# Second attention layer of a graph network: the two sums of the own rows move from GpSimd to VectorE

## The chip, the cores and the metric

One core of a Trainium2 chip runs the whole program in one launch. The metric is device time in microseconds (us). Five engines work side by side, each on its own in-order queue, and meet only at semaphores: TensorE (PE in the profile; PEld is its weight load), VectorE (DVE), ScalarE (ACT), GpSimd (POOL) and SyncE (SP, whose queue only issues transfers).

## The reference, cut to what matters

Four graph layers follow one another over 50,000 nodes of 128 features and 25,000 edges, sorted by destination. After each layer comes `x = layernorm(x + layer(x))`. The change lies in the third layer of the reference, the program's second attention layer (in the kernel `kind == 2`):

```python
q = x @ Wq + bq; k = x @ Wk + bk; v = x @ Wv + bv            # 8 heads of 16
score = einsum(q[dst], k[src]) / sqrt(16) + edge_attr @ We + be
exp_s = exp(score - segment_max(score, dst)[dst])
attn = exp_s / (segment_sum(exp_s, dst)[dst] + 1e-8)
out = segment_sum(attn * v[src], dst) @ Wo + bo
h = out + x                                                  # "own rows" are these x, one for each edge slot
layer = layernorm(h) * gamma + beta
x = layernorm(x + layer)
```

So the own row of a destination is needed twice: as `x + bo`, to which `out` is added before the first normalisation, and as `x + beta`, to which the scaled first normalisation is added before the second.

## The kernel before, in words

Nodes without edges are worked out in an early stage. The later stages work on edges in 49 chunks of 512 edge slots (`G_CH`; a chunk is a tile of 128 partitions x 512 columns, four blocks of 128 rows). Chunk L uses buffers `B[L % 5]` (`RING` is 5). The stage of `kind == 2` runs from about 2790 to 3675 us of the span, then comes a meeting of all engines and the stage of `kind == 3`, the last one.

Within a stage the order of each engine's queue is not written out by hand. Each step has a place in `plan`, and one iteration is `lag` places long (138 for this stage). `Line.run` (from L865 on) sorts the steps that an engine has by `place + lag * L` and issues them in that order. So an engine's round, in order of the place modulo 138, is in this stage:

- VectorE: `d.scale` (5), `maximum` (11), `h_res` (41), `d.stats` (50), `x3_pre` (64), `e.stats` (80), `sums` (94), `e.scale` (114), `qk` (120), `divide` (132)
- TensorE: `turn_o` (9), `turn_q` (22), `rows_o` (28), `turn_x` (38), `products` (84), `values` (101), `turn_sums` (117), `scores` (129)
- ScalarE: the copies out of PSUM, the exponentials and the applications of the normalisations
- GpSimd: `residual` (30) and `gather` (-420, over three rounds ahead)

Steps of different chunks share a round: `h_res` of chunk L runs about two rounds after `qk` of chunk L.

Steps that matter here, with the lines of the profile:

- `gather` (L900) issues eight indirect DMAs for a chunk: four of source rows (`gs`) and four of own rows (`own`). It first waits until chunk L-5 has gone through `xsT_ps`, `xdT_ps`, `xo` and `x2b`, since its buffers are written again.
- `residual` (GpSimd, L1773 and L1774) waits for the chunk's edge attributes (`ea_in`) and its gathered rows, then makes `xo = own + bo` and `w = own + beta2`. Each is a 128x512 float32 addition.
- `sums` (VectorE, L953, L957, L960) makes the messages and runs two scans, `den` and `num`.
- `turn_sums` (TensorE, L368, L1883, L965) turns `num` and `den` into rows as soon as `num` is there. `divide` (VectorE, L2023, L973, L975, L978) waits for it. L2023, the first instruction of that step, copies a few columns of chunk L-3 (`q_all`).
- `scores` (TensorE, L1856, L1858), `maximum` (VectorE, L931, L933, L935, L936, L938), `turn_o`, `turn_q` and `rows_o` (TensorE, L368, L374) follow. `h_res` (VectorE, L2039) adds `xo` to the product with `Wo` in PSUM, so it waits for `rows_o` and for `xo`. `x3_pre` (L2047, L2050) adds `w`.
- In the stage of `kind == 3` VectorE makes its own residual (L2059) as one 128x512 addition of the same form, beside gathers of GpSimd.

At the start of the stage the places put `gather` of chunks 0 to 3 ahead of `residual` of chunk 0 in GpSimd's queue.

Of the kernel before, what the change touches and what calls it, by code (L numbers as in the profile page):

```python
# [19 lines left out]
ALU = mybir.AluOpType  # L20
# [8 lines left out]
RING = 5  # L29
# [18 lines left out]
def build(nc, x, src, dst, ea32, ea64, ew, w, out):  # L48
# [65 lines left out]
    bo, gamma2, beta2 = (sb(n, [P, D]) for n in ("bo", "gamma2", "beta2"))  # L114
# [16 lines left out]
    def rows4(t):  # L131

        return t.rearrange("p (j f) -> p j f", j=SUB)

    def each_row(row):
        return row[:, None, :].to_broadcast([P, SUB, D])
# [854 lines left out]
    with ExitStack() as tmp:  # L991
# [9 lines left out]
        own = tile("own")  # L1001
# [672 lines left out]
    for kind in (2, 3):  # L1674
# [2 lines left out]
        table, ea = tables[kind + 1], (ea32 if kind == 2 else ea64)  # L1677
        if kind == 2:
            lag, plan = HOP4_LAG, {
                "load": (1, "ea_in pen_in"), "residual": (30, "xo x2b"),  # L1680
                "turn_x": (38, "xsT_ps xdT_ps eaT_ps"), "copy_xT": (66, "xsT xdT eaT"), "products": (84, "k_ps q_ps"),
                "values": (101, "v_ps"), "copy_z": (112, "kb"), "qk": (120, "qk"), "scores": (129, "z_ps"),
                "maximum": (149, "M_first M dz Dm0 Dm"), "gather": (-420, ""), "exps": (181, "p F"),
                "sums": (232, "msg den num"), "turn_sums": (255, "num_rows"), "divide": (270, "dn rd divided"),
                "turn_o": (285, "oT_ps"), "copy_oT": (296, "oT"), "rows_o": (304, "wo_ps"), "h_res": (317, "h_res"),
                **ln_plan("d", 326, 394, 419, 439), "x3_pre": (478, "dg x3_pre"), **ln_plan("e", 494, 510, 528, 547),
                "store": (565, "stored"), "turn_q": (574, "x3T_ps"), "copy_q": (592, "x3T")}
        else:
            lag, plan = HOP5_LAG, {
                "load": (1, "ea_in pen_in ew_in q_in own_in"),  # L1690
                "turn_x": (72, "xsT_ps eaT_ps"), "copy_xT": (100, "xsT eaT"), "residual": (105, "xo"), "products": (136, "z_ps"),
                "gather": (-420, ""), "values": (163, "v_ps"), "copy_z": (174, "kb"), "qk": (218, "zl"),
                "maximum": (227, "M_first M dz Dm0 Dm"), "exps": (261, "p F"), "sums": (286, "msg den num"),
                "turn_sums": (342, "num_rows"), "divide": (403, "dn rd divided"), "x4_pre": (416, "x4_pre"),
                **ln_plan("f", 474, 490, 516, 522), "scatter": (540, "")}
        new_phase()
        with ExitStack() as tmp:
            hop = Line(tmp, f"t{kind}", plan, lag, "xsT pen kb qk p F den num msg xo " + ("xdT w" if kind == 2 else "own u x4"),
                      {"gs": (table, NT + GT, slot_idx), **({"own": (table, NT + GT, own_idx)} if kind == 2 else {})})
            B = hop.B  # L1700
# [19 lines left out]
            with nc.Block() as block:  # L1720
# [41 lines left out]
                @block.gpsimd  # L1762
                def _(pool):
                    step = hop.steps()

                    if kind == 2:
                        @step("residual")
                        def _(L):

                            b = B[L % RING]  # L1770
                            step.due_dma(pool, "ea_in", L)
                            hop.due_gathered(pool, L)
                            nc.gpsimd.tensor_tensor(rows4(b["xo"][:]), rows4(b["own"][:]), each_row(bo), ALU.add).then_inc(S("xo"), 1)  # L1773
                            nc.gpsimd.tensor_tensor(rows4(b["w"][:]), rows4(b["own"][:]), each_row(beta2), ALU.add).then_inc(S("x2b"), 1)  # L1774

                    @step("gather")
                    def _(L):
                        for name in ["xsT_ps"] + ["xdT_ps", "xo", "x2b"] * (kind == 2):
                            step.due(pool, name, L, RING)
                        hop.gather(pool, L)  # L1780

                    if kind == 3:
                        @step("scatter")
                        def _(L):

                            step.due(pool, "f_out", L)
                            for t in range(SUB):
                                k = L * SUB + t
                                pool.indirect_dma_start(out=out, out_offset=bass.IndirectOffsetOnAxis(ap=end_idx[:, k:k + 1], axis=0),  # L1789
                                                        in_=B[L % RING]["x4"][:, t * D:(t + 1) * D], in_offset=None,  # L1790
                                                        bounds_check=NODES - 1, oob_is_err=False).then_inc(pool_dma[f"scattered{L % RING}"], 16)

                    step.run()
                    hop.end_gathers(pool)
                    if kind == 3:
                        for L in range(G_CH - RING, G_CH):
                            pool.wait_ge(pool_dma[f"scattered{L % RING}"], 16 * SUB * (L // RING + 1))
# [166 lines left out]
                def _(v):  # L1964
                    V = nc.vector
                    step = hop.steps()
# [64 lines left out]
                        divide(v, step, b, L, K[4], K[5], heads, 1e-8 if kind == 2 else 1e-16, b["o"])  # L2031

                    if kind == 2:
                        @step("h_res")
                        def _(L):
                            b = B[L % RING]
                            step.due(v, "wo_ps", L)
                            step.due(v, "xo", L)
                            V.tensor_tensor(b["u"][:], K[7], b["xo"][:], ALU.add).then_inc(S("h_res"), 1)  # L2039

                        ln_vector(v, step, B, "d", "u", "h_res")

                        @step("x3_pre")
                        def _(L):
                            b = B[L % RING]
                            step.due(v, "d_out", L)
                            V.tensor_tensor(rows4(b["v"][:]), rows4(b["v"][:]), each_row(gamma2), ALU.mult).then_inc(S("dg"), 1)  # L2047
                            step.due(v, "dg", L)
                            step.due(v, "x2b", L)
                            V.tensor_tensor(b["u"][:], b["v"][:], b["w"][:], ALU.add).then_inc(S("x3_pre"), 1)  # L2050

                        ln_vector(v, step, B, "e", "u", "x3_pre")
                    else:
                        @step("residual")
                        def _(L):

                            b = B[L % RING]
                            step.due_dma(v, "own_in", L)
                            V.tensor_tensor(rows4(b["xo"][:]), rows4(b["own"][:]), each_row(bias3), ALU.add).then_inc(S("xo"), 1)  # L2059

                        @step("x4_pre")
                        def _(L):
                            b = B[L % RING]
                            step.due(v, "divided", L)
                            step.due(v, "xo", L)
                            V.tensor_tensor(b["u"][:], b["o"][:], b["xo"][:], ALU.add).then_inc(S("x4_pre"), 1)

                        ln_vector(v, step, B, "f", "u", "x4_pre")
# [43 lines left out]
```

## Time and profile before

| | us |
|---|---|
| median of 3 runs | 4333.93 |
| lowest, highest | 4331.24, 4335.06 |
| the profiled execution | 4329.79 |
| its span, first to last instruction | 4328.1 |
| busy in the span: PE, DVE, ACT, POOL | 2921.5, 3475.1, 2494.4, 2522.2 |

The profiled execution is 4.14 us under the median, and 1.69 us of it lie outside the span. A busy share over the whole span mixes stages with different limits, so this table cannot say what the stage of the change waits for. For that one reads the stretch from 2790 to 3675 us alone, first by window, then by wait, then instruction by instruction. The granted clock of TensorE is a share of its full 2.4 GHz: a stretch at 0.5 runs at 1.2 GHz.

### The profile page before, as it was taken

How to read it: one execution, taken by the hardware profiler on the slowest of the kernel's cores; microseconds unless marked ns; L12 is line 12 of the kernel's file. 1: busy time of each engine (PE TensorE's matmuls, PEld its weight loads, DVE VectorE, ACT ScalarE, POOL GpSimd, SP SyncE). 2: the span in 40 equal slices, each digit the busy share in tenths (PEclk: the TensorE clock that was granted, in tenths of full speed). 3: DMA queues.
4: the chain of work that ended last, by engine and by line, in shares of the span. 5: the costliest groups of instructions: out<-in, count | busy, mean ns of one | idle time of the engine just before them, and what ended most of it. 6: DMA issues, size and time to landing. Idle time of an engine off the chain costs nothing. (4 is left out here: it accounts for less than half of the span.)

```text
span 4328.1 us, 48774 instructions
## 1 busy us (share of the span) xinstructions
PE 2921.5 (68%) x12128; PEld 1943.4 (45%) x12128; DVE 3475.1 (80%) x8069; ACT 2494.4 (58%) x5486; POOL 2522.2 (58%) x2300
## 2 busy tenths in 40 slices
PE   5777767777673178874545545478888887677775
PEld 3544444454442034444545534345555554344443
DVE  5999999999998678875656679768777776788886
ACT  3777777777776256762323334446656565455554
POOL 6655555545450166626767767588666650766664
PEclk9998898888986578777767755577777776656555
DMA  4876666555553388854444456422222220333331
GB/s 114 178 186 186 185 190 187 186 190 187 187 181 132 103 246 255 252 165 124 152 128 151 152 164 198 154 62 72 66 68 64 67 62 28 106 88 87 92 95 49
DMA packets 383765, 599.12 MB, mean 138 GB/s; under 512 B 124231, under 2 KB 205296, under 8 KB 383486
## 3 DMA queue, kind: packets, MB, share of 16 engines
q1 hardware_dynamic: 313726, 482.99, 36.5%
q0 software_dynamic: 69760, 113.02, 10.5%
q8 instruction: 101, 1.65, 0.2%
q14 instruction: 178, 1.46, 0.1%
HBM read 312.45 MB, written 287.17 MB: 139 GB/s over the span
## 5 line engine op out<-in xcount | busy, mean ns | idle before, releaser
L1555 POOL DMA_INDIRECT gs_g<-table_xw,slot_idx x588 | 593.9, 1010 | 296.9 <-issue 263.7
L900 POOL DMA_INDIRECT gs_t<-table_x,slot_idx x392 | 421.5, 1075 | 300.8 <-issue 198.5
L495 POOL DMA_INDIRECT gs<-x,src_idx x200 | 224.2, 1121 | 441.1 <-DMA xd_rows<-gd 368.8
L368 PE MATMUL ps<-ident,gs_g 128*128 128x128 f32 x588 | 137.1, 377 | 363.2 <-DMA gs_g<-table_xw,slot_idx 363.2
L1593 ACT ACTIVATE hT_g<-u_g 128x512 f32<-128x512 f32 x147 | 92.5, 629 | 497.7 <-DVE u_g L1642 497.7
L1272 POOL DMA_INDIRECT slot_idx<-node_map,src_idx x200 | 242.8, 1214 | 190.9 <-DMA slot_idx<-node_map,src_idx 94.6
L1635 DVE TENSOR_TENSOR_SCAN agg_g<-same_seg,agg_g,ps 128x512 f32<-128x512 uint8 x147 | 188.0, 1279 | 173.9 <-PE ps L368 173.6
L483 POOL DMA_INDIRECT node_map<-slot_no,end_idx x200 | 278.8, 1394 | 60.9 <-issue 60.3
L1789 POOL DMA_INDIRECT out<-x_t,end_idx x196 | 205.6, 1049 | 169.6 <-ACT x_t L339 116.9
L368 PEld LDWEIGHTS ps<-ident,gs_g 128*128 128x128 f32 x588 | 90.0, 190 | 402.6 <-issue 352.0
L495 POOL DMA_INDIRECT gd<-x,dst_idx x200 | 215.4, 1077 | 60.9 <-issue 60.0
L1848 PE MATMUL ps<-xsT_t,Wv 128*128 128x512 f32 x196 | 152.3, 870 | 133.0 <-DVE msg_t L953 132.8
L900 POOL DMA_INDIRECT own_t<-table_x,own_idx x196 | 200.3, 1022 | 59.7 <-issue 59.7
L1630 DVE SCALAR_TENSOR_TENSOR own_g<-bs_row,root,own_g 128x128 f32<-128x128 f32 x588 | 167.2, 346 | 48.7 <-DMA own_g<-table_xw 48.2
L628 ACT ACTIVATE h1T<-ps,h_bias 128x512 f32<-128x512 f32 x49 | 33.7, 687 | 268.7 <-DVE nm L775 267.9
L1940 ACT COPY xsT_t<-ps 128x512 f32<-128x512 f32 x49 | 28.7, 585 | 250.3 <-PE ps L368 250.3
L596 ACT ACTIVATE x_b<-v_b,nm,rs 128x128 f32<-128x128 f32 x392 | 156.6, 497 | 19.4 <-DVE nm L775 19.4
L596 ACT ACTIVATE x_b<-s_b,nm,rs 128x128 f32<-128x128 f32 x392 | 156.8, 497 | 17.1 <-DVE nm L775 17.1
L596 ACT ACTIVATE hf_b<-hf_b,nm,rs 128x128 f32<-128x128 f32 x392 | 157.5, 514 | 2.4 <-DVE nm L775 2.4
L596 ACT ACTIVATE x_b<-t_b,nm,rs 128x128 f32<-128x128 f32 x392 | 157.4, 510 | 0.0
L374 PE MATMUL ps<-WS,hT_g 128*128 128x128 f32 x784 | 152.9, 362 | 5.5 <-ACT xw_g L1601 5.5
L1913 ACT COPY xsT_t<-ps 128x512 f32<-128x512 f32 x98 | 56.4, 576 | 171.8 <-PE ps L368 171.8
(362 smaller groups left out, 10071.3 us busy)
## 6 DMA issues: line engine op xcount, KB each, us to landing
table_xw<-xw_b SPq DMA_DIRECT2D x147, 512.0 KB, 5.4
table_x<-x_b SPq DMA_DIRECT2D x98, 512.0 KB, 2.7
own_g<-table_xw SPq DMA_DIRECT2D x147, 256.0 KB, 3.7
x_in<-x SPq DMA_DIRECT2D x49, 512.0 KB
out<-hf_b SPq DMA_DIRECT2D x49, 512.0 KB, 2.9
table_xw<-xw_g SPq DMA_DIRECT2D x98, 256.0 KB
pen_t<-pen_row SPq DMA_DIRECT2D x98, 256.0 KB, 4.1
xd_rows<-gd SPq DMA_DIRECT2D x50, 256.0 KB, 5.6
```

The source lines that it names most:

```text
L368: last = nc.tensor.transpose(to[0:width, j * P:(j + 1) * P], t[:, j * width:(j + 1) * width], ident[:])
L374: last = nc.tensor.matmul(to[:, j * D:(j + 1) * D], tT[:, j * P:(j + 1) * P], W[:], start=True, stop=bias_row is None)
L483: pool.indirect_dma_start(out=node_map, out_offset=bass.IndirectOffsetOnAxis(ap=end_idx[:, t:t + 1], axis=0), in_=slot_no[:, t:t + 1], in_ ...
L495: pool.indirect_dma_start(out=to[k % 3][:, j * D:(j + 1) * D], out_offset=None, in_=x, in_offset=bass.IndirectOffsetOnAxis(ap=of[:, n:n + ...
L596: last = nc.scalar.activation(to[:, k * D:(k + 1) * D], of(k), ACT.Identity, scale=r[:, n, k:k + 1], bias=b[:, n, k:k + 1])
L900: pool.indirect_dma_start(out=self.B[L % RING][g][:, t * D:(t + 1) * D], out_offset=None, in_=table, in_offset=bass.IndirectOffsetOnAxis(a ...
L1272: pool.indirect_dma_start(out=slot_idx[:, t:t + 1], out_offset=None, in_=node_map, in_offset=bass.IndirectOffsetOnAxis(ap=src_idx[:, t:t + ...
L1555: pool.indirect_dma_start(out=gs[c % 6][:, j * D:(j + 1) * D], out_offset=None, in_=tables[layer], in_offset=bass.IndirectOffsetOnAxis(ap= ...
L1630: V.scalar_tensor_tensor(out=blk, in0=bs_row[layer][:], scalar=root4[:, k:k + 1], in1=blk, op0=ALU.mult, op1=ALU.add).then_inc(S("own_bias ...
L1635: V.tensor_tensor_scan(agg[t % 3][:], same_seg[:, t * CH:(t + 1) * CH], T_X[t % 2], agg[(t - 1) % 3][:, CH - 1:CH], ALU.mult, ALU.add).the ...
L1789: pool.indirect_dma_start(out=out, out_offset=bass.IndirectOffsetOnAxis(ap=end_idx[:, k:k + 1], axis=0), in_=B[L % RING]["x4"][:, t * D:(t ...
L1848: nc.tensor.matmul(K[3], (Wv if kind == 2 else Wv3)[:], B[L % RING]["xsT"][:], start=True, stop=True).then_inc(S("v_ps"), 1)
```

## The change

The step `residual` of the stage `kind == 2` goes from GpSimd's list to VectorE's list, and from place 30 to place 130. That is behind `qk` (120) and ahead of `divide` (132) in the round. It no longer waits for `ea_in`. Both semaphores are now raised by VectorE, and `gather` waits for the same ones as before.

```diff
-                "load": (1, "ea_in pen_in"), "residual": (30, "xo x2b"),
+                "load": (1, "ea_in pen_in"), "residual": (130, "xo x2b"),
...
                 def _(pool):
                     step = hop.steps()
 
-                    if kind == 2:
-                        @step("residual")
-                        def _(L):
-
-                            b = B[L % RING]
-                            step.due_dma(pool, "ea_in", L)
-                            hop.due_gathered(pool, L)
-                            nc.gpsimd.tensor_tensor(rows4(b["xo"][:]), rows4(b["own"][:]), each_row(bo), ALU.add).then_inc(S("xo"), 1)
-                            nc.gpsimd.tensor_tensor(rows4(b["w"][:]), rows4(b["own"][:]), each_row(beta2), ALU.add).then_inc(S("x2b"), 1)
-
...
                     if kind == 2:
+                        @step("residual")
+                        def _(L):
+                            b = B[L % RING]
+                            hop.due_gathered(v, L)
+                            V.tensor_tensor(rows4(b["xo"][:]), rows4(b["own"][:]), each_row(bo), ALU.add).then_inc(S("xo"), 1)
+                            V.tensor_tensor(rows4(b["w"][:]), rows4(b["own"][:]), each_row(beta2), ALU.add).then_inc(S("x2b"), 1)
+
                         @step("h_res")
```

## Rows read from the trace of the kernel before

**Rows 1.** Windows (busy by engine, PE clock, DMA share, GB/s), middle of the stage
```profile
3220.00:3320.00 100.00, 84.81 (x336) 55.48 (x336) 74.20 (x140) 60.84 (x117) 63.00 (x58) 0.73 0.25 66
```

**Rows 2.** Waits from 2850 to 3600 us: us in total, times, longest
```profile
DVE q_all L2023 <- PE ps L965: 76.5, 43, 3.4
POOL xo_t L1773 <- DMA ea<-ea: 66.0, 32, 14.6
```

**Rows 3.** Groups of VectorE, 2850 to 3600 us: busy us, mean ns, idle before
```profile
L957 DVE TENSOR_TENSOR_SCAN den_t<-F_t,den_t,p_t 128x512 f32<-128x512 f32 x44 | 59.4, 1351 | 0.0
...
L936 DVE TENSOR_TENSOR F_t<-pen_t,M_t 128x512 f32<-128x512 f32 x44 | 47.9, 1088 | 0.0
L938 DVE TENSOR_TENSOR F_t<-F_t,M_t 128x512 f32<-128x512 f32 x44 | 39.2, 891 | 1.5
```

**Rows 4.** Tile xo of both stages: ns min/median/max, first and last start
```profile
L1773 POOL TENSOR_TENSOR xo_t<-own_t,bo x49: 1256/1280/1795, 2833.6 to 3599.7; 128x512 f32<-128x512 f32 x49
...
L2059 DVE TENSOR_TENSOR xo_t<-own_t,bias x49: 681/684/693, 3700.6 to 4285.9; 128x512 f32<-128x512 f32 x49
```

**Rows 5.** Timeline of VectorE, one round: start us, us, engine, instruction, [idle before]
```profile
3269.69 1.26 DVE L960 TENSOR_TENSOR_SCAN num_t<-F_t,num_t,msg_t 128x512 f32<-128x512 f32 x1
...
3271.13 0.75 DVE L2006 SCALAR_TENSOR_TENSOR qk_t<-ps,bq,kb_t 128x512 f32<-128x512 f32 x1
3273.38 0.17 DVE L2023 COPY q_all<-ps 128x16 f32<-128x16 f32 x1 [1.50 <-PE ps L965]
```

**Rows 6.** Timeline of VectorE, the last stage's residual and what follows it
```profile
3961.49 0.68 DVE L2059 TENSOR_TENSOR xo_t<-own_t,bias 128x512 f32<-128x512 f32 x1
3962.09 0.17 DVE L329 RECIPROCAL rs_t<-sd_t 128x4 f32<-128x4 f32 x1
```

**Rows 7.** Timelines of VectorE and GpSimd, last full rounds of the stage
```profile
3595.85 0.18 DVE L973 TENSOR_SCALAR dn_t<-ps 128x32 f32<-128x32 f32 x1
...
3600.89 1.28 POOL L1774 TENSOR_TENSOR w_t<-own_t,beta 128x512 f32<-128x512 f32 x1
...
3612.90 0.18 DVE L973 TENSOR_SCALAR dn_t<-ps 128x32 f32<-128x32 f32 x1
...
3620.80 0.69 DVE L2039 TENSOR_TENSOR F_t<-ps,xo_t 128x512 f32<-128x512 f32 x1 [0.85 <-PE ps L374]
...
3629.95 0.18 DVE L973 TENSOR_SCALAR dn_t<-ps 128x32 f32<-128x32 f32 x1
```

**Rows 8.** Timelines of three engines at the start of the stage
```profile
2825.83 1.16 PE L374 MATMUL ps<-Wo,xsT_t 128*128 128x128 f32 x8 [0.68 <-ACT xsT_t L1940]
...
2827.58 0.69 DVE L938 TENSOR_TENSOR F_t<-F_t,M_t 128x512 f32<-128x512 f32 x1
...
2832.61 1.00 POOL L900 DMA_INDIRECT own_t<-table_x,own_idx  x1 [0.30 <-issue]
2833.64 1.27 POOL L1773 TENSOR_TENSOR xo_t<-own_t,bo 128x512 f32<-128x512 f32 x1
...
2835.01 0.69 DVE L2039 TENSOR_TENSOR F_t<-ps,xo_t 128x512 f32<-128x512 f32 x1 [6.74 <-POOL xo_t L1773]
```

**Rows 9.** Line L900, every gather: time from issue to landing
```profile
DMA to landing us min/median/max: 2.4/2.6/6.2
```

**Rows 10.** Timelines of GpSimd and VectorE, a long scan in the fourth round
```profile
2887.89 1.28 POOL L1773 TENSOR_TENSOR xo_t<-own_t,bo 128x512 f32<-128x512 f32 x1
...
2889.11 2.39 DVE L957 TENSOR_TENSOR_SCAN den_t<-F_t,den_t,p_t 128x512 f32<-128x512 f32 x1
```

**Rows 11.** Timeline of VectorE, the first step of divide of chunk 1
```profile
2842.23 0.19 DVE L973 TENSOR_SCALAR dn_t<-ps 128x32 f32<-128x32 f32 x1 [2.07 <-PE ps L965]
```

**Rows 12.** Timeline of VectorE, one short round and a long operation in it
```profile
3273.47 0.18 DVE L973 TENSOR_SCALAR dn_t<-ps 128x32 f32<-128x32 f32 x1
...
3278.43 1.67 DVE L938 TENSOR_TENSOR F_t<-F_t,M_t 128x512 f32<-128x512 f32 x1
...
3289.20 0.18 DVE L973 TENSOR_SCALAR dn_t<-ps 128x32 f32<-128x32 f32 x1
```

## The prediction

> **What bounds the kernel now.** Of the span of 4328.1 us only the stage of the second attention layer, from 2790 to 3675 us, is touched, so I read that stretch alone. The windows come first: in the middle of the stage TensorE is busy 85 us of 100 at a granted clock of 0.73 of 2.4 GHz, VectorE 74, GpSimd 63 [rows 1]. No engine is full, so the rounds are set by a loop through several engines. The waits show where that loop holds VectorE. VectorE waits 76.5 us for TensorE before it copies the columns of `q_all` (43 times, 1.78 each) [rows 2]. GpSimd waits 66 us for the edge attributes: it is early, and no bottleneck in the steady part [rows 2].
>
> The timeline shows the first of these waits. `num` starts at 3269.69 and takes 1.26; TensorE can only then begin `turn_sums`. VectorE has `e.scale` and `qk` meanwhile, ends `qk` at 3271.88 and stands idle for 1.50 until 3273.38 [rows 5]. From the twelfth round on no round has less than this 1.50, and most have just that. That gap is the place to which the change moves the two additions.
>
> The round takes 17.05 us at the end of the stage, twice in a row (3595.85, 3612.90, 3629.95), and over the 46 rounds from 2842.23 to 3629.95 it is 787.72 / 46 = 17.12 on average [rows 7, 11]. Single rounds go from 15.7 (3273.47 to 3289.20) [rows 12] to about 18: TensorE alternates between its two clock levels, 1.2 and 2.4 GHz, within each round.
>
> **The change part by part.**
>
> *Added on VectorE, steady part.* Two 128x512 additions for each of 49 chunks. The nearest row is the same instruction form in the last stage: 681 to 693 ns, median 684, beside gathers [rows 4]. There the next instruction starts 0.60 after it [rows 6]. So two cost about 0.60 + 0.68 = 1.28 us per round: 49 x 1.28 = 63 us of VectorE work. It lies after `qk`. The first starts at about 3271.80, the second ends at about 3273.08, and the copy wanted by 3273.38 is not late: 0.3 us are left. On the path: 0. This cover is TensorE's `turn_sums`. If it were gone, up to 63 us would appear. The lower bound of the cost is 0 (additions cannot shorten the wait); the upper one comes from L936 and L938, which take up to about 1.0 longer when GpSimd adds at the same time [rows 12]: 2 x 1.0 less the 0.3 left is 1.7 a round, 78 us. I take 0, because the nearest row, L2059, never exceeds 693 ns and GpSimd no longer adds; the end of 78 needs an addition on GpSimd that the change removes, so only a small part of it enters the range.
>
> *Removed from GpSimd, steady part.* 98 additions of 1.28 us [rows 4], some 125 us of an engine that is early. On the path: 0 by itself. But they lengthen VectorE's work. L936 has a mean of 1088 ns and L938 of 891, against 690 undisturbed [rows 3, 8]; L957 has 1351, against 1260 of the like scan L960 [rows 3, 5]. Over 44 rounds that is 17.5 + 8.8 + 4.0, some 30 us. Does that reach the path? In most rounds not. After `maximum` VectorE waits for `rows_o` anyway. The round from 3612.90 to 3629.95 has no addition on GpSimd at all (the last one starts at 3600.89), and VectorE then simply waits 0.85 for L374. That round is 17.05 long, as is the one before it, which does have one [rows 7]. So this stage's locked round is worth the same with and without the disturbance. The exception is a disturbance behind `h_res`, where `num` waits for VectorE: in the fourth round L957 takes 2.39 beside the addition that starts at 2887.89 [rows 10], 1.1 over the 1.26 of L960 [rows 5]. I count it: -1.1. Unknown are the rounds with the fast clock, as the one in which L938 takes 1.67, 1.0 too long [rows 12]: there `rows_o` is done before VectorE. By the timelines `h_res` starts 0.1 to 1.8 us after `rows_o` in 19 rounds, 10 us in sum. I take 0, by the two rounds of [rows 7]; the bounds are -10 (all of it is regained) and +3 (the mixed rounds, on average 16.99 from the twelfth on, all lock at 17.05).
>
> *The queue at the start.* Before, the residual of chunk 0 stands behind 32 gathers on GpSimd, the last of which starts at 2832.61; `xo` starts at 2833.64, and `h_res` of chunk 0 waits for it for 6.74 us, to 2835.01. Everything else that it needs was there earlier: `rows_o` ended at 2826.99, VectorE's L938 at 2828.27 [rows 8]. In the new order the addition follows `qk` of chunk 0, long before. So -6.7 us. What is late next? `turn_x` of chunk 3 stands behind `turn_sums`, `scores` and `rows_o` of chunk 1; `divide` of chunk 1, which starts at 2842.23 before, would start at about 2835.5, and those two come after it. The last rows of chunk 3 are issued by 2833.6 and land 2.6 us later, at 2836.2 [rows 8, 9, 11]. Not late.
>
> *Moved waits.* The step drops its wait for `ea_in` and keeps that for the gathers, which on VectorE is long fulfilled: TensorE turned the same rows before `qk`. Queued behind it is `divide`, hence `turn_o`, so it would matter if it waited. GpSimd's gathers now wait for VectorE's `x2b` instead of their own engine; they need 8 x 1.3 = 10.4 us of a round of 17 [rows 8] and run over three rounds ahead, so 0. SyncE's queue is unchanged.
>
> *Sum.* -6.7 - 1.1 = -7.8 us. The profiled execution would go from 4329.8 to 4322.0. The median stands 4.1 above that execution, so I forecast 4333.9 - 7.8 = 4326 us as the median.
>
> *A rule against it.* The trace shows the lengthened operations, and the last stage shows none beside gathers [rows 3, 4]. The Trainium skill (SBUF — State Buffer, Who interferes with whom) says that a VectorE instruction with two SBUF inputs contends with a GpSimd instruction that reads SBUF, and that the loser blocks fully. By that, the two additions, which have two SBUF inputs each, would be exposed if gathers counted as such readers; the L2059 row says they don't, and the measurement decides.
>
> **The rivals.** A measurement of this kernel can tell about 0.2% (8.7 us) from no change.
>
> *Kept, but more (20%).* The relief on VectorE does reach the rounds with the fast clock. Then the 10 us above come on top: 4326 - 10 = 4316. For it: such rounds start `h_res` as soon as L938 is done. Against it: the clock takes part in the length of the round, and the two undisturbed rounds are no shorter.
>
> *Given back by the clock (9%).* The idle time of TensorE at the start is gone, its slow phases come earlier, and the rounds that follow grow by what was gained: 4334. For it: the rounds from the third to the fifth were already the longest of the stage. Against it: the long scan in the fourth is one reason [rows 10].
>
> *The gap is too small (8%), the slower side.* The two additions end after the time at which `q_all` can be copied (3273.38 in [rows 5]). The two additions would have to take 1.6 us instead of 1.28; from that point every further tenth costs 46 x 0.1 = 4.6 us. With 1.9 that is 14 us, less the gain of 7.8: about 4340. For it: the margin is thin. Against it: the spread of L2059 is 12 ns.
>
> *The clock rule (5%).* What TensorE does before its clock falls is a stretch of short turns with gaps, and before it rises a stretch of long products; if fewer gaps kept it at 2.4 GHz, all rounds would go to the 15.7 of [rows 12]: 46 x 1.4 = 64 us less, 4262. The Trainium skill (TensorE: Matmul & The Clock Gate, What's actually happening) states such a rule: activity releases the throttle, idleness brings it back. Against it stand the undisturbed rounds at 17.05, in which TensorE's gaps are latencies that the change leaves alone.
>
> **How the numbers follow.** The forecast has 58%. Its own range is 4321 to 4331, for the start's gain may be kept in part, and one or two more disturbed rounds may count. Range over all cases: 4313 to 4339; it holds the forecast, most of the larger gain, the give-back and part of the slower case. Faster by over 0.2% needs 8.7 us: nearly half of the forecast's share (0.22), the larger gain (0.18) and the clock case (0.05), 0.45. Within 0.2%: the rest of the forecast and the give-back, 0.46. Slower: 0.09.
>
> **What the new profile would show.** The wait of `h_res` on `xo` at the start is gone and L2039 of chunk 0 starts near 2828. The idle time before L2023 falls from 1.50 to about 0.3 in the steady rounds, with its start unchanged against `num`. L936 and L938 have means of about 690, L957 one of about 1270. VectorE's busy time rises by about 63 - 33 = 30 us (33 being the 30 above over all 49 chunks), GpSimd's falls by about 125. L973 still comes every 17.0 to 17.1 us. The forecast is wrong if the idle time before L2023 vanishes and the round grows, if the mean round falls below 16.9, or if the first rounds after 2842 take longer than before.

## The result and the profile after

The median went from 4334.5 to 4301.0 us (four runs each), a ratio of 0.9919 with a 95% interval of 0.9904 to 0.9934: 33.5 us faster, where I had forecast 8. The forecast of 4326 and its range down to 4313 were both missed, on the fast side. The profiled span is 30.0 us shorter (4298.1 against 4328.1).

The page of the kernel after, part 1 (busy us, share, instructions):

```profile
span 4298.1 us, 48725 instructions
...
PE 2886.4 (67%) x12128; PEld 1920.0 (45%) x12128; DVE 3496.7 (81%) x8167; ACT 2495.2 (58%) x5486; POOL 2394.1 (56%) x2202
```

VectorE is 21.6 us busier and GpSimd 128.1 less. TensorE is 35.1 us less busy with the same instructions, and its granted clock over the span is 0.748 against 0.740, so it ran more of them at 2.4 GHz. The windows answer to [rows 1] and show where:

```profile
2800.00:2860.00 60.00, 47.30 (x203) 28.74 (x204) 48.16 (x83) 33.14 (x59) 46.90 (x44) 0.87 0.22 59
2860.00:2920.00 60.00, 45.78 (x210) 27.95 (x210) 51.65 (x98) 40.12 (x76) 46.75 (x44) 0.87 0.32 87
3220.00:3320.00 100.00, 87.72 (x351) 56.24 (x350) 80.81 (x156) 61.55 (x120) 50.68 (x47) 0.72 0.26 67
```

The same first two windows of the kernel before:

```profile
2800.00:2860.00 60.00, 42.57 (x146) 24.05 (x146) 32.12 (x51) 22.58 (x39) 47.81 (x45) 0.76 0.16 45
2860.00:2920.00 60.00, 51.16 (x181) 33.23 (x180) 44.50 (x77) 31.32 (x60) 50.25 (x45) 0.67 0.28 77
```

In the middle of the stage little differs (0.72 against 0.73). At its start the granted clock is 0.87 instead of 0.67 to 0.76, and VectorE gets through 83 and 98 instructions where it had 51 and 77. The waits from 2850 to 3600 us (us in total, times, longest) answer to [rows 2]:

```profile
POOL gs_t L900 <- DVE w_t L2029: 200.6, 33, 7.7
...
DVE q_all L2013 <- PE ps L965: 32.8, 45, 1.5
...
DVE F_t L2036 <- PE ps L374: 24.0, 29, 0.9
```

The wait for `q_all` fell from 76.5 to 32.8: the additions fill it. GpSimd waits for `w_t` instead of edge attributes. VectorE now waits 24.0 us, 29 times, for `rows_o`; before it was 8.0 us, 17 times, because a lengthened operation often came later than `rows_o`. The groups of VectorE in that stretch (busy us, mean ns, idle before) answer to [rows 3], and the tile `xo` to [rows 4]:

```profile
L957 DVE TENSOR_TENSOR_SCAN den_t<-F_t,den_t,p_t 128x512 f32<-128x512 f32 x45 | 57.3, 1274 | 0.0
...
L938 DVE TENSOR_TENSOR F_t<-F_t,M_t 128x512 f32<-128x512 f32 x45 | 31.3, 695 | 1.6
...
L936 DVE TENSOR_TENSOR F_t<-pen_t,M_t 128x512 f32<-128x512 f32 x44 | 30.1, 684 | 0.0
```

```profile
L2028 DVE TENSOR_TENSOR xo_t<-own_t,bo x49: 679/681/684, 2807.2 to 3598.4; 128x512 f32<-128x512 f32 x49
```

None of these operations is lengthened any more. VectorE's busy time rose by 21.6 where the additions alone are 63, so some 41 us of lengthening are gone. A part of it stands in no row of the prediction, on the small L332 of the normalisations, which reads two small tiles. The groups of VectorE from 2850 to 3600 us, before and after:

```profile
L332 DVE SCALAR_TENSOR_TENSOR nm_t<-st_t,rs_t 128x4 f32<-128x4 f32 x88 | 21.4, 243 | 3.0
```

```profile
L332 DVE SCALAR_TENSOR_TENSOR nm_t<-st_t,rs_t 128x4 f32<-128x4 f32 x89 | 14.4, 162 | 3.0
```

The timeline of VectorE shows the start, which answers to [rows 8, 11] (`h_res` is now L2036), and then the gap of [rows 5]:

```profile
2824.04 0.69 DVE L938 TENSOR_TENSOR F_t<-F_t,M_t 128x512 f32<-128x512 f32 x1
2824.65 0.68 DVE L2036 TENSOR_TENSOR F_t<-ps,xo_t 128x512 f32<-128x512 f32 x1
...
2830.91 0.18 DVE L973 TENSOR_SCALAR dn_t<-ps 128x32 f32<-128x32 f32 x1
...
3262.25 0.18 DVE L973 TENSOR_SCALAR dn_t<-ps 128x32 f32<-128x32 f32 x1
...
3276.93 0.75 DVE L1996 SCALAR_TENSOR_TENSOR qk_t<-ps,bq,kb_t 128x512 f32<-128x512 f32 x1
3277.60 0.68 DVE L2028 TENSOR_TENSOR xo_t<-own_t,bo 128x512 f32<-128x512 f32 x1
3278.20 0.68 DVE L2029 TENSOR_TENSOR w_t<-own_t,beta 128x512 f32<-128x512 f32 x1
3279.18 0.17 DVE L2013 COPY q_all<-ps 128x16 f32<-128x16 f32 x1 [0.30 <-PE ps L965]
3279.27 0.18 DVE L973 TENSOR_SCALAR dn_t<-ps 128x32 f32<-128x32 f32 x1
```

`h_res` of chunk 0 follows L938 at once. In this round of the steady part the idle time is 0.30 where it was 1.50, and the round takes 17.02, close to the 17.05 of [rows 7]. It isn't so in every round: of the first 45 copies of `q_all` 23 wait 0.30 or 0.31, and 9 still wait 1.50 or 1.51. So the shape of the forecast is there in part, and the gain lies elsewhere. I read it off the starts of L973 (round n reaches from `divide` of chunk n to the next):

| us, profiled execution | before | after | difference |
|---|---|---|---|
| start of the stage | 2794.6 | 2792.8 | -1.8 |
| from there to `divide` of chunk 0 | 28.1 | 26.3 | -1.8 |
| round 0 | 19.6 | 11.8 | -7.8 |
| rounds 1 to 4 | 73.0 | 59.0 | -14.0 |
| rounds 5 to 46 | 714.7 | 710.2 | -4.5 |
| rounds of 16.9 to 17.2 among these 42 | 6 | 17 | |
| rounds over 17.2 among these 42 | 21 | 12 | |

Over two thirds of the gain of this pair lies in the first five rounds. After the change those run at 2.4 GHz for most of their length: the granted clock over them is 0.93, against 0.71 before. A second execution of the changed kernel, `c_after` below, puts it less sharply: 72.3 us for rounds 0 to 4 and 703.3 for rounds 5 to 46. Of its 34.7 us of shorter span 20.3 lie in the first five rounds and 11.4 in the later ones. So two executions of one kernel differ by 7 us in the later rounds, and a few us there can't be read from one trace.

### The profile page after: what moved, and what is told of

Its sections match the earlier page's. It is cut to its first block and busy times, and to the rows that moved or that the text cites. A ratio compares the mean times of both kernels' runs of the same rounds, so it can differ in the third digit from the quotient of the medians.

```text
span 4298.1 us, 48725 instructions
## 1 busy us (share of the span) xinstructions
PE 2886.4 (67%) x12128; PEld 1920.0 (45%) x12128; DVE 3496.7 (81%) x8167; ACT 2495.2 (58%) x5486; POOL 2394.1 (56%) x2202
## 3 DMA queue, kind: packets, MB, share of 16 engines
q0 software_dynamic: 69760, 113.02, 10.8%
## 5 line engine op out<-in xcount | busy, mean ns | idle before, releaser
L900 POOL DMA_INDIRECT gs_t<-table_x,slot_idx x392 | 408.8, 1043 | 465.7 <-DVE w_t L2029 200.6
L900 POOL DMA_INDIRECT own_t<-table_x,own_idx x196 | 215.4, 1099 | 59.7 <-issue 59.7
L596 ACT ACTIVATE x_b<-s_b,nm,rs 128x128 f32<-128x128 f32 x392 | 156.8, 497 | 17.1 <-DVE nm L775 17.1
L374 PE MATMUL ps<-WS,hT_g 128*128 128x128 f32 x784 | 152.2, 360 | 4.3 <-ACT xw_g L1601 4.3
```

The costliest lines, as they stand in the source:

```text
L374: last = nc.tensor.matmul(to[:, j * D:(j + 1) * D], tT[:, j * P:(j + 1) * P], W[:], start=True, stop=bias_row is None)
L596: last = nc.scalar.activation(to[:, k * D:(k + 1) * D], of(k), ACT.Identity, scale=r[:, n, k:k + 1], bias=b[:, n, k:k + 1])
L900: pool.indirect_dma_start(out=self.B[L % RING][g][:, t * D:(t + 1) * D], out_offset=None, in_=table, in_offset=bass.IndirectOffsetOnAxis(a ...
```

## The experiments

**The question.** Two effects can have made the first rounds short: the wait of `h_res` at the start is gone, with all that follows from it (TensorE's clock included), or GpSimd's additions no longer lengthen operations of VectorE. The expectations below call the first theory A and the second theory B, and each of them as recorded has one of the two do nearly all of it. The other answers were that both count, and that the amount of GpSimd's work matters rather than its place.

Only some series ran on a chip on which the kernel before takes 4335 us; in the others every kernel takes 4519 to 4637 and scatters more. Each ratio is against runs of the kernel before on the same chip.

| run | median, us | before, us | ratio, 95% |
|---|---|---|---|
| c_after | 4300.6 | 4336.7 | 0.9922 (0.9905 to 0.9938) |
| r1_order_only | 4324.0 | 4336.7 | 0.9975 (0.9965 to 0.9984) |
| r2_stall_kept | 4313.5 | 4336.7 | 0.9948 (0.9933 to 0.9963) |
| r3_both | 4420.3 | 4336.7 | 1.0186 (1.0166 to 1.0206) |
| e1_order_only | 4578.8 | 4597.2 | 0.9966 (0.9936 to 0.9997) |
| e2_stall_kept | 4595.8 | 4597.2 | 1.0009 (0.9982 to 1.0036) |
| e3_both | 4636.6 | 4597.2 | 1.0103 (1.0017 to 1.0188) |
| e4_first_six | 4613.6 | 4597.2 | 1.0042 (1.0021 to 1.0063) |
| r4_first_six | 4580.1 | 4557.4 | 1.0045 (1.0022 to 1.0068) |
| r5_first_six | 4577.8 | 4563.5 | 1.0031 (1.0006 to 1.0057) |
| e8_gap_pool | 4519.5 | 4557.4 | 0.9923 (0.9899 to 0.9947) |
| r8_gap_pool | 4525.1 | 4563.5 | 0.9919 (0.9892 to 0.9946) |
| r9_gap_pool | 4559.4 | 4586.2 | 0.9922 (0.9892 to 0.9951) |
| e10_both_gap | 4527.0 | 4557.4 | 0.9941 (0.9923 to 0.9959) |
| e6_double | 4571.7 | 4557.4 | 1.0033 (1.0013 to 1.0053) |
| r6_double | 4570.1 | 4563.5 | 1.0026 (0.9995 to 1.0056) |
| c2_after | 4554.4 | 4563.5 | 0.9975 (0.9948 to 1.0003) |
| e11_three_ahead | 4550.9 | 4586.2 | 0.9913 (0.9883 to 0.9942) |

### The order alone, and the stall alone

*Order only*: the additions stay on GpSimd and only their place in its queue changes, so that chunk 0's stand ahead of the gathers of chunk 3 (the first addition comes after 24 gathers instead of 32).

```diff
 (against the kernel before)
-"residual": (30, "xo x2b"),
+"residual": (-10, "xo x2b"),
```

> The kernel before, with the additions still on GpSimd and only their place moved from 30 to -10, so that the residual of chunk 0 stands ahead of the gathers of chunk 3 in GpSimd's queue. Theory A (the wait at the start lets TensorE's clock fall, and the rounds after it pay): h_res of chunk 0 no longer waits, the first five rounds shrink as in the changed kernel, 20 to 28 us less than before, 4306 to 4314. Theory B (GpSimd's additions lengthen VectorE's operations, and that is what costs in rounds with the fast clock): the additions still collide, only the 6.7 us of the wait are gained, about 4327, with rounds 2 to 5 still at 17 to 20 us.

*Stall kept*: the changed kernel, in which `h_res` of chunk 0 waits for the gathers of chunk 3, as it did before through GpSimd's queue.

```diff
 (against the kernel after)
                             step.due(v, "xo", L)
+                            if L == 0:
+                                hop.due_gathered(v, 3)
```

> The changed kernel, but h_res of chunk 0 also waits for the gathers of chunk 3, which puts the old wait of 6 to 8 us back with no addition on GpSimd. Theory A: 20 to 28 us of the gain are lost with it, 4321 to 4329, and rounds 1 to 5 are 16.5 to 20 us long. Theory B: only the wait itself comes back, 6 to 8 us, about 4308, and rounds 2 to 5 stay at 14 to 15.5.

Both ran again on the chip that takes 4335, with the changed kernel beside them:

> The changed kernel itself, as the measure for the other kernels of this series. The first series ran where the kernel before took about 4597 us, with idle times of 10 to 28 us at the start of the stage and longer early stages in every kernel of it, so its total times can't be set beside 4334 and 4301. Both theories: 0.8% less than before, here too; round 1 to 5 in sum under 62 us, mean of the 46 rounds 16.7.

> As e1_order_only, again: additions on GpSimd at place -10. Theory A (the start and the clock): 20 to 28 us less than before, rounds 1 to 5 in sum near 60. Theory B (GpSimd's additions lengthen VectorE's operations): 5 to 9 us less than before, rounds 1 to 5 in sum near 70, mean round 17.1.

> As e2_stall_kept, again: changed kernel plus the old wait of h_res of chunk 0. Theory A: 20 us or more above the changed kernel. Theory B: only 6 to 8 us above it, mean round 16.7, as the trace of the first series already had it (16.76).

By the ratios the order alone is worth 0.25%, 10.8 us. Without GpSimd's additions but with the stall it is 0.52%, 22.5 us. Their sum, 33.3, is the 33.8 of `c_after`: both effects count, and they add up. The replayed stall is a little longer than the original (8.36 against the 6.74 of [rows 8]). So the wait is worth 11 to 13 us and GpSimd's additions 21 to 23, each known to 4 to 7 us either way by the intervals. A single cause falls, and with it both expectations: theory A asked for 20 to 28 us from the order alone, theory B for 5 to 9, and it was 11 to 13; `r2_stall_kept` should have been 20 or more, or 6 to 8, above the changed kernel, and it was 13 (4313.5 against 4300.6).

One round in which they part is plain in `r1_order_only`. Its timelines, all engines, where the additions meet VectorE:

```profile
2886.73 1.06 PE L374 MATMUL ps<-Wo,xsT_t 128*128 128x128 f32 x8
...
2887.59 3.32 DVE L938 TENSOR_TENSOR F_t<-F_t,M_t 128x512 f32<-128x512 f32 x1
2887.86 1.27 POOL L1773 TENSOR_TENSOR xo_t<-own_t,bo 128x512 f32<-128x512 f32 x1
2889.10 1.25 POOL L1774 TENSOR_TENSOR w_t<-own_t,beta 128x512 f32<-128x512 f32 x1
...
2890.83 0.68 DVE L2039 TENSOR_TENSOR F_t<-ps,xo_t 128x512 f32<-128x512 f32 x1
```

`rows_o` ends at 2887.79, but `h_res` starts 3.0 us later, because L938 takes 3.32 in place of 0.69. The round lasts 18.29. The same round of the changed kernel lasts 15.38. L374 tells a part of why this did not show in the rounds I had judged by. One row of each, the last rounds of the kernel before and an early round of the changed kernel:

```profile
3618.85 1.91 PE L374 MATMUL ps<-Wo,xsT_t 128*128 128x128 f32 x8
```

```profile
2848.45 1.06 PE L374 MATMUL ps<-Wo,xsT_t 128*128 128x128 f32 x8
```

At 1.2 GHz `rows_o` takes 1.91 and ends after VectorE is done, so VectorE has 0.85 to spare and a short collision hides in it. At 2.4 GHz it takes 1.06, VectorE is the one that is waited for, and a lengthened L936 or L938 delays `h_res`.

That isn't the whole price, though. Here are the later rounds of five executions on the faster chip, sorted by how long their `rows_o` takes:

| rounds 5 to 46 | in sum, us | `rows_o` 1.06: rounds, mean us | `rows_o` 1.91: rounds, mean us |
|---|---|---|---|
| before | 714.7 | 9, 16.92 | 33, 17.04 |
| `r1_order_only` | 724.7 | 17, 17.37 | 25, 17.18 |
| `r2_stall_kept` | 706.6 | 17, 16.71 | 25, 16.90 |
| after | 710.2 | 13, 17.07 | 29, 16.84 |
| `c_after` | 703.3 | 19, 16.77 | 23, 16.73 |

Against the changed kernel `r1_order_only` loses 6 to 7 us in rounds 1 to 4 (66.3 against 59.0 and 60.5) and 15 to 21 in rounds 5 to 46. So most of the additions' price is spread over the stage. And the rounds with a `rows_o` of 1.91 are longer too (17.18 against 16.84 and 16.73), so not every collision hides there. Some are longer than the 0.85 (the longest L936 of the kernel before takes 2.46). How the price splits between these, the operations behind `h_res` and the clock is not shown.

On the slower chip the order alone gave about as much (0.9966), but `e2_stall_kept` gave nothing against the kernel before. It is no test of the stall: the stage started so late there that chunk 3's rows had landed, and `h_res` of chunk 0 waited 0.53 us for TensorE instead of 8.36 for the gathers. The section on the slower chips takes up why it started late.

### The additions on both engines

*Both*: the changed kernel, and GpSimd makes the two additions too, at the old place, into scratch tiles that nobody reads.

```diff
 (against the kernel after)
+"extra": (30, "extra0 extra1"),
...
+step.due_dma(pool, "ea_in", L)
+hop.due_gathered(pool, L)
+step.due(pool, "extra1", L, 1)
+nc.gpsimd.tensor_tensor(rows4(extra[0][:]), rows4(b["own"][:]), each_row(bo), ALU.add)...
+nc.gpsimd.tensor_tensor(rows4(extra[1][:]), rows4(b["own"][:]), each_row(beta2), ALU.add)...
```

> The changed kernel with both additions on VectorE as changed, and beside them the same two additions on GpSimd as before (place 30, same waits) into scratch tiles that nobody reads; only the gathers wait for them. The collisions are back, the wait at the start is not. Theory A: within 4 us of the changed kernel, about 4301 to 4305. Theory B: most of the gain beyond the wait is lost, 20 us more than changed, about 4320 to 4326, with L936, L938 or L957 again up to 1 us longer.

> As e3_both, again: changed kernel plus the same additions on GpSimd into scratch tiles. Theory A: within 4 us of the changed kernel. Theory B: 20 us or more above it; the trace of the first series had a mean round of 18.24, which would be 70 us.

It was 120 us slower than the changed kernel (4420.3 against 4300.6), far more than the 22 that the collisions cost before. The groups of VectorE from 2850 to 3560 us:

```profile
L957 DVE TENSOR_TENSOR_SCAN den_t<-F_t,den_t,p_t 128x512 f32<-128x512 f32 x36 | 68.5, 1902 | 0.0
L2055 DVE TENSOR_TENSOR p_t<-p_t,gamma 128x512 f32<-128x512 f32 x36 | 62.0, 1721 | 0.0
L936 DVE TENSOR_TENSOR F_t<-pen_t,M_t 128x512 f32<-128x512 f32 x35 | 26.0, 743 | 0.0
L938 DVE TENSOR_TENSOR F_t<-F_t,M_t 128x512 f32<-128x512 f32 x35 | 24.3, 695 | 1.2
```

The collisions have moved. They now fall on the scan of `den` and on the product with gamma, between `h_res` and `num`, where nothing hides them: 0.63 + 1.05 more per round. The mean round is 19.63, which is 3.0 more than in `c_after`. The traced execution took 4443.7, 23 over the median of its kernel, and what makes up the rest is open. What a collision costs depends on where it falls. The experiment therefore shows the mechanism but does not price what the change removed, which I had wanted of it.

### GpSimd's work kept, only its phase moved

*Gap*: the kernel before, but the additions stay on GpSimd and are released by `qk` of VectorE, so that they run in the gap where VectorE waits for TensorE.

```diff
 (against the kernel before)
-"residual": (30, "xo x2b"),
+"residual": (-10, "xo x2b"),
...
-step.due_dma(pool, "ea_in", L)
+step.due(pool, "qk", L)
```

> The kernel before, additions still on GpSimd, at place -10 as in r1_order_only, but released by VectorE's qk of the same chunk instead of by ea_in, so that they run in VectorE's gap ahead of q_all and its PSUM operations, and not beside the operations with two SBUF inputs. If the collisions with VectorE are the larger part of the gain (theory B, by the last series 21 us, beside 11 to 13 us for the wait at the start): all of it is there without moving the work, 4298 to 4306, mean round 16.6 to 16.8, L936, L938 and L957 undisturbed. If it is the amount of work on GpSimd, or its queue, that costs: as r1_order_only, about 4324.

> As e8_gap_pool, again: additions on GpSimd, released by qk. Its rounds were 16.67 us on average, as the changed kernel's. If collisions are all that is left beside the start: within 6 us of the changed kernel (4296 to 4306, where before takes 4335); if moving the work off GpSimd matters by itself: 4320.

> As e8_gap_pool, a third time, to set it beside e11_three_ahead and, where before takes 4335, beside the changed kernel: ratio 0.990 to 0.993 on either chip. If moving the work off GpSimd matters by itself beyond the collisions, 0.996 or more where before takes 4335.

Three runs, in three series on the slower chips, gave 0.9923, 0.9919 and 0.9922, with every addition still on GpSimd. That is the ratio which the change itself has on the faster chip (0.9922), where this kernel was not run. Beside it in one series on a slower chip (`r8_gap_pool`, `c2_after`) the changed kernel had only 0.9975, because of the late start described below. The groups of `e8_gap_pool`, 3100 to 3780 us:

```profile
L957 DVE TENSOR_TENSOR_SCAN den_t<-F_t,den_t,p_t 128x512 f32<-128x512 f32 x41 | 52.2, 1273 | 0.0
...
L938 DVE TENSOR_TENSOR F_t<-F_t,M_t 128x512 f32<-128x512 f32 x41 | 28.4, 692 | 1.4
...
L936 DVE TENSOR_TENSOR F_t<-pen_t,M_t 128x512 f32<-128x512 f32 x41 | 28.3, 689 | 0.0
...
L2023 DVE COPY q_all<-ps 128x16 f32<-128x16 f32 x40 | 7.0, 174 | 80.5 <-PE ps L965 80.5
```

Hardly any operation is lengthened, and the wait for `q_all` is as long as before or longer (80.5). The mean rounds are 16.67, 16.78 and 16.76 in the three, against 17.23 in `e1_order_only`, which differs from this kernel only in what releases the additions. The changed kernel has 16.72 and 16.61 on the faster chip and 16.45 in `c2_after`. So most of what the rounds gain comes from when the additions run; that the engine and GpSimd's load count for nothing is not shown. With both engines adding the phase decides too:

*Both, in the gap*: "both" with `extra` at place 131 and released by `x2b` in place of `ea_in`.

> As r3_both, with the extra additions of GpSimd released by x2b (behind VectorE's own additions) at place 131. Same work on every engine as r3_both, only another phase. Theory B: the 120 us that r3_both lies above the changed kernel fall to under 15, 4301 to 4315, L957 back at 1275 and the product with gamma (1721 ns in r3_both) at 675. If the amount of work on GpSimd costs: stays near 4420.

The ratio is 0.9941, where `e3_both` had 1.0103 on another of the slower chips. L957 is back at 1274 and the product with gamma at 674, in the groups of VectorE from 3100 to 3780 us:

```profile
L957 DVE TENSOR_TENSOR_SCAN den_t<-F_t,den_t,p_t 128x512 f32<-128x512 f32 x40 | 51.0, 1274 | 0.0
...
L2055 DVE TENSOR_TENSOR p_t<-p_t,gamma 128x512 f32<-128x512 f32 x40 | 26.9, 674 | 0.0
L332 DVE SCALAR_TENSOR_TENSOR nm_t<-st_t,rs_t 128x4 f32<-128x4 f32 x80 | 26.6, 332 | 2.7
```

What is left is on the small L332: 332 ns on average, 163 in `e8_gap_pool`. The traced execution took 4550.8, 24 over the median of its kernel.

### More additions on VectorE

*Double*: the changed kernel with two more additions per chunk in VectorE's step, into scratch.

```diff
 (against the kernel after)
+step.due(v, "extra", L, 1)
+V.tensor_tensor(rows4(extra[0][:]), rows4(b["own"][:]), each_row(bo), ALU.add)
+V.tensor_tensor(rows4(extra[1][:]), rows4(b["own"][:]), each_row(beta2), ALU.add)...
```

> The changed kernel with two more additions of the same kind in the same step, into scratch tiles: 1.2 us more for VectorE in the gap. If the gap of 1.50 covers the first pair with 0.3 left, as said: 0.9 us on the path in rounds that wait for TensorE there, 1.2 where the wait is already 0; 46 rounds give 40 to 55 us, 4340 to 4355. If the clock or another wait absorbs it: under 20 us.

> As e6_double, again: 1.2 us more of additions for VectorE in the gap. 0.9 to 1.2 us a round if it all lies on the path, 40 to 55 us above the changed kernel. The trace of the last series had a mean round of only 16.96, which would be 12 to 16 us; so my expectation now is 12 to 20 above the changed kernel, the rest being taken up by the clock, which has more of the round at full speed when TensorE has waited.

`r6_double` takes 4570.1 against 4554.4 for `c2_after` beside it: 15.7 us for 49 x 1.28 = 63 us of work. With 0.30 left in the gap of every round, 0.98 a round or 45 us would have shown; a third did. The waits from `divide` of chunk 1 to that of chunk 47 in `c2_after` and `r6_double` say why:

```profile
DVE q_all L2013 <- PE ps L965: 39.5, 41, 2.2
```

```profile
DVE q_all L2014 <- PE ps L965: 1.7, 6, 0.3
```

The gap of the changed kernel is not 0.30 everywhere: it still holds 39.5 us there, and the second pair fills 38 of them. That leaves 25 of the 63 us, and the 46 rounds grew by 19 (mean 16.86 against 16.45). That the clock would take up the rest, as expected, does not show: granted were 0.76 over rounds 5 to 46 of `r6_double` and 0.82 in `c2_after`. So a pair of additions costs little while it fits in the gap, which fits the 0 of the forecast for the first pair without measuring it.

### The first six chunks only

*First six*: additions of chunks 0 to 5 on VectorE (place 130), all others on GpSimd (place 30).

> Additions on VectorE for chunks 0 to 5 alone, for chunks 6 to 48 on GpSimd as before. If the gain lies in the first rounds (theories A and B both say so, from rounds 1 to 5 that fell from 73.0 to 59.0 us in sum and the first from 19.6 to 11.8): 21 to 26 us less than before, 4308 to 4313. If it is spread over the whole stage: only about a quarter, 4324 to 4328.

> As e4_first_six, again: additions on VectorE for chunks 0 to 5, on GpSimd from 6 on. If most of the gain lies in the first rounds (sum of rounds 0 to 5 fell from 92.6 to 70.8 and 72.3 us): 20 to 25 us less than before, 4311 to 4317. If the collisions cost evenly over all rounds: 11 for the wait and a tenth of 21, about 13 us less, 4324.

> As e4_first_six, again: VectorE for chunks 0 to 5, GpSimd from 6 on. Rounds 0 to 5 took 71.3 us in sum in the last series, as in the changed kernel, and the later ones 17.2, as before. So 18 to 24 us less than before, 4311 to 4317 where before takes 4335.

All three missed their expectation: they are slower than the kernel before (1.0031 to 1.0045), not 18 to 26 us faster. In `r4_first_six` the rounds 0 to 4 take 71.2 us, like the changed kernel's 70.8, but in `e4_first_six` and `r5_first_six` they take 80.4 and 82.1. The later rounds run at 17.28, 17.23 and 17.20 (17.02 in the kernel before on the faster chip). In the series of `r5_first_six` the changed kernel needs 695.8 us for rounds 5 to 46, this one 722.3 (one execution of each). So on this chip the later rounds gain much from the change, and a gain confined to the start is not what it has there. The ratio itself says little, since the stage starts late here too (next section), and no trace shows how the kernel before starts on such a chip.

### The slower chips: a gap at the start

> The changed kernel, as the measure of this series. Where the kernel before takes about 4335: ratio 0.992 again. Where it takes 4560 or more: its rounds are as short (mean 16.6 to 16.8), but the idle times marked issue at the start, seen in the other kernels with additions on VectorE from chunk 0 on, may take the gain back; a ratio of 0.992 to 1.001.

The changed kernel gained only 0.25% there. From the start of the stage to `divide` of chunk 0 it took 75 us, where `r8_gap_pool` took 38. The timelines of VectorE and GpSimd in `c2_after`:

```profile
3024.38 0.75 DVE L1996 SCALAR_TENSOR_TENSOR qk_t<-ps,bq,kb_t 128x512 f32<-128x512 f32 x1 [12.05 <-issue]
...
3060.12 0.75 DVE L1996 SCALAR_TENSOR_TENSOR qk_t<-ps,bq,kb_t 128x512 f32<-128x512 f32 x1 [22.09 <-issue]
...
3085.96 0.19 DVE L973 TENSOR_SCALAR dn_t<-ps 128x32 f32<-128x32 f32 x1 [23.89 <-DMA out<-hf_b]
```

```profile
3080.19 1.00 POOL L900 DMA_INDIRECT own_t<-table_x,own_idx  x1 [0.30 <-issue]
3098.84 0.99 POOL L900 DMA_INDIRECT gs_t<-table_x,slot_idx  x1 [17.65 <-DVE w_t L2029]
```

GpSimd issues 56 gathers from 3007 to 3081 us without a pause, and VectorE stands still three times. The first of these waits, 11 to 15 us long, is there in every run, on the faster chip too (12.5 in the kernel before, 12.2 after). The other two, 46 us, are what is new. With the additions on GpSimd the early gathers are broken by them. The kernels that make no addition there (`e2`, `e4`, `e6` and `r6`, `r4`, `r5`, `c2_after`) all take 71 to 76 us to the first `divide`; those with additions on GpSimd from the start (`e1`, `e8`, `r8`, `r9`, `e10`, `e3`) 38 to 46. To test it, gathers were held back to three chunks ahead:

```diff
 (against the kernel after, in the step gather)
+if kind == 2:
+    step.due(pool, "x2b", L, 3)
```

> The changed kernel, with the gathers of chunk L also waiting for x2b of chunk L-3, so that GpSimd pauses after three chunks at the start instead of running on. If the unbroken gathers hold up the other engines' start where before takes 4560: the 50 us of idle time shrink to about 10 and the ratio goes from 0.9975 to about 0.990 to 0.992. If not: 0.9975. Where before takes 4335 there is no such idle time: 0.992, as the changed kernel.

The time to the first `divide` fell to 44 us, the mean round to 16.11, and the ratio is 0.9913. The traced execution took 4513.5, 37 under the median of its kernel, so the 16.11 is not typical of the kernel. GpSimd now pauses early, after 32 gathers:

```profile
3060.72 0.99 POOL L900 DMA_INDIRECT gs_t<-table_x,slot_idx  x1 [6.32 <-DVE w_t L2031]
```

So a pause in the run of gathers takes most of the gap at the start away, and I hold the unbroken run responsible. By which means it acts no view names: of the two new waits one is put down to nothing, the other to a transfer of another stage. A rival would be the loading of the engines' own code behind the gathers; the DMA views of `c2_after` list no packet of an instruction queue from 3050 to 3090 us, which speaks against it without ruling it out. The start of the kernel before was not traced on such a chip. On the chip that takes 4335 the same run does no harm (26 us to the first `divide`). The interval of `e11_three_ahead` overlaps that of `r9_gap_pool` beside it (0.9922), so it is not shown to be the better of the two; against the changed kernel there are only the ratios of two series (0.9913 and 0.9975, whose intervals are apart), no run side by side. On the chip that takes 4335 it was not run.

## Why the prediction was wrong, by its own steps

**Added on VectorE: 0.** Not contradicted. The additions take 679 to 684 ns, they fill a wait whose total fell by 43.7 us, and in the profiled execution no copy of `q_all` waits less than 0.18. That they cost exactly 0 no run isolates.

**Removed from GpSimd: -1.1.** This is the step that failed: "I take 0, by the two rounds of [rows 7]". By the runs the term is 21 to 23 us. The prediction calls both rounds undisturbed, but in the first L936 takes 1.22, and `h_res` still waits 0.31 for `rows_o`; only the second, from 3612.90, is free of additions. Both are 17.05 long, at a granted clock of 0.70 and with a `rows_o` of 1.91, and they stood for 46 rounds that go from 15.6 to 20.4. They say nothing of rounds in which `rows_o` takes 1.06, nor of collisions longer than 0.85, nor of those behind `h_res`, of which the prediction counted one (1.1) out of the 4.0 that it had worked out for L957. L332, lengthened by some 7 us in all, was in none of its terms.

The bound of -10 was not only too tight, it was the price of something else. It took the delay of `h_res` behind `rows_o`, 10 us in 19 rounds. After the change that delay is much the same: 8.5 us in 17 rounds, and 11.3 in 22 rounds of `c_after`. It belongs to rounds in which `rows_o` takes 1.06, disturbed or not, and of those there are 9 among rounds 1 to 46 before and 17 and 22 after. Which operations and how much of the clock make up the 21 to 23 stays open.

**A rule against it.** The Trainium skill (SBUF — State Buffer, Who interferes with whom) has a VectorE instruction with two SBUF inputs contend with a GpSimd instruction that reads SBUF, the later one blocking fully. The trace agrees for additions as to which pairs collide: L936, with two SBUF inputs, has 1088 ns before and 684 after, while L935, which reads PSUM, has 691 in both. It agrees on the blocking too: L938 ends in `r1_order_only` only after both of GpSimd's (3.32 against 1.27 + 1.25 + 0.69). It does not show that the later one is the blocked one: by the profile L938 starts at 2887.59, 0.27 before GpSimd's first addition, and is held all the same. Against gathers it doesn't occur here (679 to 684 ns), as the forecast had it.

**The queue at the start: -6.7.** The mechanism was right and the size short. The wait of 6.74 is gone, and nothing was late next. Round 0 shrank by 7.8. By the runs the removal is worth 11 to 13. The rounds after it keep the 2.4 GHz that they had lost behind the stall (windows at 0.87 and 0.87 against 0.76 and 0.67; with the stall replayed in `r2_stall_kept`, 0.74 and 0.74). Which part of it is the clock no run isolates.

**Moved waits: 0.** Nothing on the chip of the forecast speaks against it. On the slower chips it was wrong: GpSimd, relieved of the additions, issues its first gathers without a break, and the stage starts some 35 us late.

**The rivals.** "Kept, but more" came nearest in kind, priced at 10 for 22, and its 4316 covers only half of the gain. "Given back by the clock" had the sign wrong: the early rounds became the fastest of the stage. The gap was not too small. All rounds at 15.7, the clock rule's case, did not come: rounds 0 to 4 are at or under that at a granted clock of 0.93, but 17 of the 42 later ones are at 17.

**The checks I had named.** The durations came out as written (L936 684, L938 695, L957 1274, GpSimd -128). VectorE rose by 21.6 for 30, most of the difference being the 7 of L332, and the idle time before the copy of `q_all` is at 0.3 in about half of the rounds. "L973 still comes every 17.0 to 17.1 us" did not: the mean of the 46 rounds is 16.72, under the 16.9 that I had set as the mark of a wrong forecast.

## What to carry to other kernels

When two engines collide, move one of them in time before moving its work: releasing GpSimd's additions by VectorE's `qk` gave 0.8% on the slower chips, for two edited lines, where the change itself gave 0.25% beside it and 0.8% on the faster chip. Do not judge a lengthened operation by rounds in which something else is late; sort the rounds by who waits for whom first, at each clock level, and price each sort by itself, with every operation that is lengthened, the small ones too. And when work leaves a queue, look at what now runs there without a break.

## What the hardware showed that I had not expected

- Two additions of GpSimd back to back hold one VectorE operation for both: 3.32 us for L938, 3.22 for the product with gamma in `r3_both` (2.5 for a pair of additions, 0.7 for itself).
- 56 indirect gathers in a row on GpSimd (74 us) went with new idle times of 22 and 24 us on VectorE at the start of a stage on the slower chips, and with none on the faster one. With a pause after the 32nd the time to the first `divide` was 31 us shorter (44 against 75, on two of the slower chips).
- Chips differ by 5 to 6% in the time of this kernel, and the same change is worth 0.8% on one and 0.25% on another.
- The mean round of `e11_three_ahead`, 16.11, is the shortest seen, with 23 of 42 later rounds under 16, in an execution that took 37 us less than the median of its kernel. Why it keeps so many short rounds stays open.
